# An attention loop in which the next batch's preparation runs three more steps ahead

## The chip, the cores and the metric

The kernel runs on one core of one Trainium2 chip. The metric is the device time of one execution in microseconds (us); lower is better. Engines are named as the profile names them: PE (TensorE; PEld is its weight loading), DVE (VectorE), ACT (ScalarE), POOL (GpSimd), SP (the queue that starts DMAs).

## What is computed

Six blocks on x of shape (4, 512, 128), in the order A B A C D C: a mixture of experts (A), eight layers of linear attention (B), A again, an attention block with its own experts (C), a state-space scan (D), and C once more. The change touches the attention in C, which runs twice:

```python
h = _layernorm(_layernorm(x), ln1_w, ln1_b)
h = causal depthwise convolution of h, 3 taps
q, k, v = split(h @ attn_w)               # 16 heads of width 8
q = q * cos + rotate_half(q) * sin        # the same for k
scores = where(causal, q @ k.T / sqrt(8), -1e30)
p = softmax(scores)
x = x + (p @ v) @ proj_w                  # then a norm and 4 experts
```

## The kernel before

Every engine has its own instruction stream, written out by hand, and engines wait for one another on semaphores. In the attention (lines 1245 to 1770) each of the 4 batches has two kinds of work.

**Side work** prepares a batch: 60 products of PE that take turns on two PSUM banks (`side`, line 1289 on), where product n waits until what lay in its bank two products before has been read. For each of the four query tiles i of 128 rows: `qkv` i; then DVE turns the positions in (`rope`, L1626 to L1633, among it the copy of v into the values' operand `vc`, L1629) and splits the numbers into bf16 pieces (`rest` L1638, `part3` L1644 and L1646), ACT rounds (`part` 1 and 2, L1417), POOL copies pieces (`spread` 1: three copies; `spread` 2: two copies). PE then transposes `key` i and `query` i (8 transposes each, L1314); ACT copies the keys (`copied`, L1427) and half of the queries (`odd_queries`, L1434), DVE the other half (`queries`, L1651). `max` products (L1325, L1329) fill a bank with scores, whose row maxima DVE takes (`maxima`, L1660): 4 for tile 0, 8 for tile 1, 16 each for tiles 2 and 3. With the maxima (`max_rows`) PE transposes the queries once more (`again` i), and ACT copies them.

**Main work** goes in 16 steps j (head group j // 4, key tile k = j % 4): `scores` (L1345) of 512 - 128 k columns in two halves on four banks, `exps` on ACT (L1479, two instructions), `select` on POOL (L1581, two), `values` on PE (L1355). A half of `scores` waits for the `exps` of the step before, which reads the same banks; `exps` j waits for `values` j - 2; `values` j waits for both `select` of j. After each group ACT copies the sums (`summed`, L1487), for which the first `values` of the next group wait; `turned` on PE, `normed` and `added_back` on DVE finish a batch.

While batch b's main work runs, the side work of batch b + 1 is dealt out over its 16 steps: side step j (a fixed list on each engine) goes with main step j. Batch 0's side work runs alone ahead of the loop, and batch 3's main work has none beside it but parts of the norm that follows. The order within a step before:

- PE: `scores` j + 1, side step j, `values` j, `turned`
- ACT: `exps` j, `summed`, side step j
- POOL: both `select` of j, side step j
- DVE: `normed`, side step j

Of the kernel before, what the change touches and what calls it, by code (L numbers as in the profile page):

```python
# [13 lines left out]
P = 128  # L14
# [41 lines left out]
def build(nc, x_in, pack_a, pack_b, pack_c, params, consts, out, stages="ABACDC"):  # L56
    par_at, par_cols = columns(PARAMS)
    con_at, con_cols = columns(CONSTS)
    with ExitStack() as ctx:
# [92 lines left out]
        vc = [view(4096 + 2048 * s, TPB, HEADS, 32) for s in range(2)]  # L152
        kt_s = [view16(8192 + 2048 * s, PAIRS, SEQ) for s in range(2)]
# [1121 lines left out]
        USES_BY_STEP = [2, 4, 9, 13, 18, 23, 26, 29, 37, 43, 47, 49, 55, 59, 60, 60]  # L1275
# [12 lines left out]
        def pe_attention(pe, c):  # L1288
# [60 lines left out]
            def values(b, j):  # L1349
# [3 lines left out]
                pe.wait_ge(S["sel_ok"], 32 * q + 2 * j + 2)  # L1353
                for m in range(4):
                    mm = pe.matmul(ps[32 * m:32 * m + 32, 4, k * P:SEQ], vc[b % 2][:, k, 4 * g + m, :],  # L1355
                                   pt[:, (2 * j + m // 2) % NPT, m % 2, 0:SEQ - k * P], start=(k == 0),
                                   stop=(k == TPB - 1), skip_group_check=True)
# [17 lines left out]
            pe.wait_ge(S["pad_ok"], c["attn"] + 1)  # L1375
            for n in range(USES):
                side(0, n)
            pe.wait_ge(S["ln_out"], 4 * c["ln"] + NB)
            scores(0, 0)
            for b in range(NB):  # L1380
                for j in range(STEPS):
                    if j + 1 < STEPS:
                        scores(b, j + 1)
                    if b + 1 < NB:
                        for n in range(USES_BY_STEP[j - 1] if j else 0, USES_BY_STEP[j]):
                            side(b + 1, n)
                        if j + 1 == STEPS:
                            scores(b + 1, 0)
                    values(b, j)
                    if b == LATE:  # L1390
# [16 lines left out]
        def act_attention(act, c):  # L1407
# [30 lines left out]
            def side(b, j):  # L1438
# [3 lines left out]
                elif j == 1:  # L1442
                    part(b, 0, 2)
                    part(b, 1, 2)
                    if b == 0:
                        act_first(act, c, 3)
                    copied(b, "key", 0)
                    odd_queries(b, 0)
                elif j == 2:
                    part(b, 2, 1)  # L1450
                elif j == 3:
                    part(b, 2, 2)
                    copied(b, "key", 1)
                    odd_queries(b, 1)
                    copied(b, "again", 0)
                elif j == 4:
                    part(b, 3, 1)
                elif j == 5:
# [3 lines left out]
                elif j == 6:  # L1462
                    copied(b, "again", 1)
                elif j == 8:
                    copied(b, "key", 3)
                    odd_queries(b, 3)
                elif j == 10:
                    copied(b, "again", 2)
                elif j == 14:
# [32 lines left out]
            for j in range(STEPS):  # L1502
                side(0, j)
                if j < NB - 1:
# [714 lines left out]
```

## Time and profile before

| | us |
|---|---|
| median of 3 runs | 2120.73 |
| lowest and highest of them | 2113.12, 2126.63 |
| the profiled execution | 2111.17 |
| its span, first to last instruction | 2109.4 |

The profile is that of one execution. Its span is cut below into stretches of the first attention: the side work of one batch ends with the transposes of `again` 3, and the stretch from there to the end of the next batch's `again` 0 is called a head here; the stretch from that `again` 0 to that batch's `again` 3 a body. So a round of the loop is a body and a head. Busy times of an engine add up its instructions without overlap; the clock is the mean share of full speed that TensorE was granted.

### The profile page before, as it was taken

How to read it: one execution, taken by the hardware profiler on the slowest of the kernel's cores; microseconds unless marked ns; L12 is line 12 of the kernel's file. 1: busy time of each engine (PE TensorE's matmuls, PEld its weight loads, DVE VectorE, ACT ScalarE, POOL GpSimd, SP SyncE). 2: the span in 40 equal slices, each digit the busy share in tenths (PEclk: the TensorE clock that was granted, in tenths of full speed). 3: DMA queues.
4: the chain of work that ended last, by engine and by line, in shares of the span. 5: the costliest groups of instructions: out<-in, count | busy, mean ns of one | idle time of the engine just before them, and what ended most of it. 6: DMA issues, size and time to landing. Idle time of an engine off the chain costs nothing.

```text
span 2109.4 us, 24691 instructions
## 1 busy us (share of the span) xinstructions
PE 1770.9 (84%) x8806; PEld 1110.2 (53%) x8806; DVE 1530.9 (73%) x2489; ACT 1334.9 (63%) x2121; POOL 654.1 (31%) x731
## 2 busy tenths in 40 slices
PE   8999798898898889996677789995776677777998
PEld 6887466665566558883233326881222232232786
DVE  6888687778787668878666545875998855664686
ACT  6998577767777679995355565556544345556554
POOL 1444111101111014445422231221898522223131
PEclk9999899999999979998899999997899679999999
DMA  3221000000000003210000001100000000000110
GB/s 100 75 76 52 15 18 18 1 18 18 18 18 11 0 13 104 70 61 15 1 1 1 1 1 46 65 1 9 3 3 32 0 1 1 1 1 1 56 56 21
DMA packets 23770, 52.89 MB, mean 25 GB/s; under 512 B 2336, under 2 KB 6816, under 8 KB 23648
## 3 DMA queue, kind: packets, MB, share of 16 engines
q1 hardware_dynamic: 23648, 51.30, 7.7%
q8 instruction: 71, 1.16, 0.2%
q14 instruction: 51, 0.42, 0.1%
HBM read 49.66 MB, written 1.64 MB: 24 GB/s over the span
## 4 chain that ended last, share of the span: by engine, by line
PE 56%; DVE 22%; ACT 16%; issue 4%; POOL 2%; DMA 1%; POOLq 0%; ACTq 0%; DVEq 0%; SPq 0%
PE ps L553 9%; PE ps L555 9%; PE ps L554 9%; DVE arena L1940 5%; DVE arena L1660 5%; PE ps L1355 3%; PE ps L782 3%; PE ps L785 3%; PE ps L1325 3%; ACT arena L1479 2%; PE ps L783 2%; PE ps L1314 2%; ACT arena L1427 2%; PE ps L1345 2%; DVE arena L1931 1%
## 5 line engine op out<-in xcount | busy, mean ns | idle before, releaser
L664 DVE TENSOR_TENSOR hid_lo<-arena,hid_hi 128x512 fp32r<-128x512 f32 x384 | 339.3, 896 | 66.9 <-ACT arena L613 65.4
L1660 DVE TENSOR_REDUCE arena<-ps 128x1 f32<-128x512 f32 (+3 forms) x352 | 213.4, 639 | 87.3 <-PE ps L1329 84.4
L553 PE MATMUL ps<-x_hi,w_hi 128*128 128x512 f32 x512 | 209.9, 410 | 2.0 <-DVE arena L756 2.0
L1581 POOL TENSOR_SCALAR_AFFINE_SELECT arena<-arena 128x256 f32<-128x256 f32 x256 | 108.2, 430 | 314.2 <-ACT arena L1479 311.7
L554 PE MATMUL ps<-x_lo,w_hi 128*128 128x512 f32 x512 | 204.0, 398 | 0.0
L555 PE MATMUL ps<-x_hi,w_lo 128*128 128x512 f32 x512 | 204.0, 398 | 0.0
L610 ACT ACTIVATE hid_hi<-ps,wslot 128x512 fp32r<-128x512 f32 x256 | 177.3, 693 | 33.7 <-PE ps L555 6.3
L1479 ACT ACTIVATE arena<-ps 128x1024 f32<-128x1024 f32 (+3 forms) x256 | 166.2, 705 | 50.0 <-PE ps L1345 49.5
L1325 PE MATMUL ps<-arena 128*128 128x512 bf16 (+3 forms) x512 | 133.7, 327 | 69.4 <-DVE arena L1660 37.8
L613 ACT ACTIVATE arena<-ps,wslot 128x512 f32<-128x512 f32 x256 | 175.0, 684 | 0.0
L1427 ACT ACTIVATE arena<-ps 128x1024 bf16<-128x1024 bf16 x64 | 65.5, 1024 | 149.8 <-PE ps L1314 149.7
L634 POOL TENSOR_TENSOR x<-x,arena 128x512 f32<-128x512 f32 x64 | 108.5, 1699 | 145.8 <-DVE arena L625 145.8
L553 PE MATMUL ps<-hid_hi,w_hi 128*128 128x512 f32 x384 | 151.6, 395 | 2.1 <-DVE hid_lo L664 2.1
L555 PE MATMUL ps<-hid_hi,w_lo 128*128 128x512 f32 x384 | 151.7, 395 | 0.0
L554 PE MATMUL ps<-hid_lo,w_hi 128*128 128x512 f32 x384 | 150.4, 392 | 0.0
L1957 POOL TENSOR_TENSOR arena<-arena 128x512 f32<-128x512 f32 x64 | 136.1, 2166 | 44.4 <-ACT arena L1882 44.4
L735 ACT ACTIVATE arena<-ps 128x512 f32<-128x512 f32 x128 | 76.4, 597 | 97.4 <-PE ps L555 97.3
L1325 PEld LDWEIGHTS ps<-arena 128*128 128x128 bf16 x512 | 42.6, 101 | 161.6 <-DVE arena L1660 98.6
L1345 PE MATMUL ps<-arena 50*128 50x256 bf16 (+3 forms) x512 | 68.3, 321 | 60.6 <-ACT arena L1479 58.0
L756 DVE TENSOR_TENSOR arena<-arena,ps 128x512 f32<-128x512 f32 x128 | 87.4, 683 | 38.6 <-ACT arena L735 38.5
L1355 PE MATMUL ps<-arena 128*32 128x512 f32 (+3 forms) x1024 | 109.1, 501 | 7.1 <-POOL arena L1581 5.1
L553 PEld LDWEIGHTS ps<-x_hi,w_hi 128*128 128x128 f32 x512 | 98.3, 192 | 29.3 <-DVE arena L756 5.2
(309 smaller groups left out, 4190.7 us busy)
## 6 DMA issues: line engine op xcount, KB each, us to landing
arena<-gates_dram SPq DMA_DIRECT2D x96, 256.0 KB, 3.5
wslot<-pack_a SPq DMA_DIRECT2D x16, 514.5 KB, 3.8
wslot<-pack_b SPq DMA_DIRECT2D x8, 900.5 KB, 4.6
wslot<-pack_c SPq DMA_DIRECT2D x8, 768.0 KB, 4.5
res<-x_in SPq DMA_DIRECT2D x4, 256.0 KB, 5.0
out_dram<-res SPq DMA_DIRECT2D x4, 256.0 KB, 2.9
con<-consts_dram SPq DMA_DIRECT2D x1, 559.0 KB, 3.9
bc_dram<-arena SPq DMA_DIRECT2D x1, 384.0 KB, 3.2
```

Source lines behind the costliest of these rows:

```text
L553: pe.matmul(ps[:, bank, :], w1, hi, start=start, stop=False)
L554: pe.matmul(ps[:, bank, :], w1, lo, start=False, stop=False)
L555: return pe.matmul(ps[:, bank, :], w2, hi, start=False, stop=stop)
L610: act.activation(hid_hi[item % 2][:, k, :], ps[:, k, :], ACT.Gelu, bias=bias)
L613: act.activation(hid32[:, k, :], ps[:, k, :], ACT.Gelu, bias=bias).then_inc(S["hi_ok"], 1)
L664: dve.tensor_tensor(hid_lo[item % 2][:, k, :], hid32[:, k, :], hid_hi[item % 2][:, k, :].bitcast(F32), ALU.subtract).then_inc(S["hid_ok"], 1)
L1325: pe.matmul(ps[:, bank, m * keys:(m + 1) * keys], qt_s[h % 2][:, h // 2, i * P:(i + 1) * P], kt_s[b % 2][:, h // 2, 0:keys], start=(m == 0 ...
L1345: mm = pe.matmul(ps[:, 2 * r + jj, 0:n], kt_s[b % 2][r0:r0 + MROWS, hp, k * P:(k + 1) * P], q2_s[b % 2][r0:r0 + MROWS, hp, k * P:SEQ], sta ...
L1355: mm = pe.matmul(ps[32 * m:32 * m + 32, 4, k * P:SEQ], vc[b % 2][:, k, 4 * g + m, :], pt[:, (2 * j + m // 2) % NPT, m % 2, 0:SEQ - k * P], ...
L1479: act.activation(pt[:, u % NPT, :, 0:n], ps[:, 2 * r:2 * r + 2, 0:n], ACT.Exp, scale=SCALE).then_inc(S["exp_ok"], 1)
L1660: dve.tensor_reduce(neg_max[:, i, heads[0]:heads[-1] + 1:step], ps[:, bank, 0:len(heads) * keys].rearrange("p (m k) -> p m k", k=keys), AX ...
L1957: pool.tensor_tensor(ch[:, s, t, :], hst[:, s, t, :], c_s[:, u % 2, :], ALU.mult).then_inc(S["ch_ok"], 1)
```

## The change

On every engine side step j + 3 goes with main step j, so that the last three main steps of a batch carry side steps 0, 1 and 2 of the batch after the next, and side steps 0 to 2 of batch 1 run ahead of the loop. Side work of batch b + 2 thus begins while batch b's values are still in use, for which the values' operand gets a third buffer, in the norm's `rstd`; POOL fills its unused columns after the convolution. The side lists are dealt out a little differently over the steps. The new order within a step (`ahead` gives side step j + 3):

- PE: `scores` j + 1, `values` j, side step j + 3, `turned`
- ACT: `summed`, `exps` j + 1, side step j + 3; `exps` 0 of a batch comes behind the last side step of the batch before
- POOL: both `select` of j, side step j + 3
- DVE: `normed`, side step j + 3

```diff
+        vc.append(rstd[:, :, :].rearrange("p i (h d) -> p i h d", d=32))
...
-        USES_BY_STEP = [2, 4, 9, 13, 18, 23, 26, 29, 37, 43, 47, 49, 55, 59, 60, 60]
+        USES_BY_STEP = [2, 2, 5, 9, 13, 18, 23, 26, 29, 36, 41, 44, 48, 53, 58, 60]
+        LEAD = 3
+
+        def ahead(b, j):
+
+            return [(b + 1 + (j + LEAD) // STEPS, (j + LEAD) % STEPS)] if b + 1 + (j + LEAD) // STEPS < NB else []
...
+                if (b, j) == (2, 0):
+                    pe.wait_ge(S["pad_ok"], 2 * c["attn"] + 2)
...
+            for j in range(STEPS):
+                side_step(0, j)
+            side_step(1, 0)
             pe.wait_ge(S["ln_out"], 4 * c["ln"] + NB)
             scores(0, 0)
+            for j in range(1, LEAD):
+                side_step(1, j)
             for b in range(NB):
                 for j in range(STEPS):
                     if j + 1 < STEPS:
                         scores(b, j + 1)
-                    if b + 1 < NB:
-                        for n in range(USES_BY_STEP[j - 1] if j else 0, USES_BY_STEP[j]):
-                            side(b + 1, n)
-                        if j + 1 == STEPS:
-                            scores(b + 1, 0)
+                    elif b + 1 < NB:
+                        scores(b + 1, 0)
                     values(b, j)
+                    for at in ahead(b, j):
+                        side_step(*at)
...
                 elif j == 1:
                     part(b, 0, 2)
                     part(b, 1, 2)
-                    if b == 0:
-                        act_first(act, c, 3)
+                elif j == 2:
                     copied(b, "key", 0)
                     odd_queries(b, 0)
-                elif j == 2:
                     part(b, 2, 1)
                 elif j == 3:
                     part(b, 2, 2)
+                elif j == 4:
                     copied(b, "key", 1)
...
+            side(1, 0)
             for b in range(NB):
+                exps(b, 0)
+                if b == 0:
+                    for j in range(1, LEAD):
+                        side(1, j)
                 for j in range(STEPS):
-                    exps(b, j)
                     if j % TPB == 0 and 4 * b + j // TPB:
                         if j:
                             summed(b, j // TPB - 1)
                         else:
                             summed(b - 1, 3)
+                    if j + 1 < STEPS:
+                        exps(b, j + 1)
                     if b and j == 4:
                         y_turned(b - 1)
-                    if b + 1 < NB:
-                        side(b + 1, j)
-                    else:
+                    for at in ahead(b, j):
+                        side(*at)
...
-            SPREAD_BY_STEP = {0: [(0, 1), (1, 1)], 1: [(0, 2), (1, 2)], 2: [(2, 1)], 3: [(2, 2)], 4: [(3, 1)], 5: [(3, 2)]}
+            SPREAD_BY_STEP = {0: [(0, 1), (1, 1)], 1: [(0, 2), (1, 2)], 2: [(2, 1)], 3: [(2, 2)], 5: [(3, 1)], 6: [(3, 2)]}
...
+            pool.memset(vc[2][:, :, :, DH:DH + 1], 1.0)
+            pool.memset(vc[2][:, :, :, DH + 1:32], 0.0).then_inc(S["pad_ok"], 1)
+            side(1, 0)
+            for j in range(1, LEAD):
+                side(1, j)
...
-                if i == 0 and q >= 2:
-                    dve.wait_ge(S["pv_mm"], 16 * (q - 1))
+                if i == 0 and b == 3:
+                    dve.wait_ge(S["pv_mm"], 16 * (q - 2))
...
-                dve.tensor_copy(vc[b % 2][:, i, :, 0:DH], ps[:, bank, 2 * P:3 * P].rearrange("p (h d) -> p h d", d=DH))\
+                dve.tensor_copy(vc[b % 3][:, i, :, 0:DH], ps[:, bank, 2 * P:3 * P].rearrange("p (h d) -> p h d", d=DH))\
...
                 elif j == 1:
                     part3(b, 0)
                     part3(b, 1)
-                    if b == 0:
-                        dve_second(dve, c, 1)
+                elif j == 2:
                     queries(b, 0)
-                elif j == 2:
                     rope(b, 2)
+                elif j == 3:
                     maxima(b, 0, range(4))
                     rest(b, 2)
                     max_rows(b, 0)
-                elif j == 3:
+                elif j == 4:
                     part3(b, 2)
                     queries(b, 1)
                     rope(b, 3)
...
-                if j < 2:
-                    dve_first(dve, c, j + 2)
-                elif j < 4:
-                    dve_second(dve, c, j)
+                if j in (0, 2):
+                    dve_first(dve, c, 2 + j // 2)
+                elif j in (1, 3, 4):
+                    dve_second(dve, c, {1: 1, 3: 2, 4: 3}[j])
+            for j in range(LEAD):
+                side(1, j)
```

The rest of the lists moves the same way, to side steps one later than before (`key`, `query` and `again` 1 from 3 to 4, `key` 3 from 8 to 9), with at most 5 maxima in a step.

## Rows read from the trace of the kernel before

**Rows 1.** First line of the page: the span of the profiled execution.
```profile
span 2109.4 us, 24691 instructions
```

**Rows 2.** Busy times by stretch, first attention: stretch, length, engines (instructions), clock, DMA.
```profile
1022.35:1047.52 25.17, 17.09 (x116) 7.46 (x120) 12.19 (x36) 12.36 (x19) 8.03 (x23) 0.80 0.00 1
1047.52:1092.60 45.08, 34.16 (x292) 13.90 (x296) 29.61 (x60) 23.84 (x34) 10.23 (x27) 0.96 0.00 1
1092.60:1117.28 24.68, 17.10 (x136) 8.06 (x140) 12.74 (x38) 13.40 (x22) 8.79 (x25) 0.86 0.00 1
1117.28:1163.98 46.70, 36.07 (x298) 14.45 (x302) 30.30 (x61) 24.33 (x35) 10.24 (x27) 0.96 0.01 1
1163.98:1188.84 24.86, 17.21 (x137) 8.10 (x140) 12.77 (x38) 13.40 (x22) 8.80 (x25) 0.86 0.00 1
1188.84:1234.24 45.40, 34.61 (x298) 14.20 (x302) 30.17 (x61) 24.33 (x35) 10.24 (x27) 1.00 0.00 1
1234.24:1236.15 1.91, 1.00 (x13) 0.31 (x12) 0.00 (x0) 1.58 (x4) 0.51 (x2) 1.00 0.00 0
1236.15:1276.41 40.26, 32.45 (x232) 9.96 (x230) 13.87 (x27) 29.29 (x49) 15.89 (x33) 0.87 0.00 1
```

**Rows 3.** Timeline in head 1: start, us, engine, line, count, [idle <-releaser].
```profile
1097.72 0.42 DVE L1626 TENSOR_TENSOR arena<-ps,con 128x256 f32<-128x256 f32 x1 [5.27 <-PE ps L1302]
...
1098.77 0.43 DVE L1633 TENSOR_TENSOR arena<-arena 128x256 f32<-128x256 f32 x1
...
1100.65 0.42 ACT L1417 ACTIVATE arena<-arena 128x256 bf16<-128x256 f32 x1 [1.00 <-DVE arena L1633]
1100.97 1.49 ACT L1479 ACTIVATE arena<-ps 128x768 f32<-128x768 f32 x2
1101.12 0.66 POOL L1558 COPY arena<-arena 128x256 bf16<-128x256 bf16 x1 [0.36 <-ACT arena L1417]
...
1101.82 0.35 PE L1345 MATMUL ps<-arena 50*128 50x256 bf16 x2 [2.50 <-ACT arena L1479]
1102.21 0.77 POOL L1581 TENSOR_SCALAR_AFFINE_SELECT arena<-arena 128x256 f32<-128x256 f32 x2
```

**Rows 4.** Waits within 1094.5 to 1165.9: engine, line, releaser, us in total, times, longest.
```profile
DVE arena L1660 <- PE ps L1329: 11.9, 13, 3.0
...
PE ps L1345 <- ACT arena L1479: 7.9, 10, 2.5
```

**Rows 5.** Groups by line, 1094.5 to 1165.9: count, busy us, mean ns, idle before.
```profile
L1581 POOL TENSOR_SCALAR_AFFINE_SELECT arena<-arena 128x256 f32<-128x256 f32 x33 | 13.2, 409 | 41.8 <-ACT arena L1479 41.5
...
L1479 ACT ACTIVATE arena<-ps 128x1024 f32<-128x1024 f32 x9 | 8.8, 1022 | 2.3 <-PE ps L1345 2.3
...
L1427 ACT ACTIVATE arena<-ps 128x1024 bf16<-128x1024 bf16 x8 | 8.2, 1024 | 17.3 <-PE ps L1314 17.3
...
L1487 ACT ACTIVATE arena<-ps 128x512 f32<-128x512 f32 x4 | 2.4, 605 | 0.0
...
L1638 DVE TENSOR_TENSOR arena<-arena 128x256 f32<-128x256 f32 x4 | 1.8, 440 | 0.1
```

**Rows 6.** Timeline of PE in body 2, at the full clock.
```profile
1139.88 1.20 PE L1314 MATMUL ps<-ident,arena 128*128 128x128 bf16 x16
...
1143.28 1.06 PE L1355 MATMUL ps<-arena 128*32 128x512 f32 x8
```

**Rows 7.** Timeline of PE in head 1 (the last row after the clock is back).
```profile
1103.77 1.81 PE L1314 MATMUL ps<-ident,arena 128*128 128x128 bf16 x15
1105.51 1.51 PE L1355 MATMUL ps<-arena 128*32 128x384 f32 x8
...
1115.58 0.91 PE L1302 MATMUL ps<-par,res 128*128 128x384 f32 x2 [0.67 <-ACT arena L1427]
```

**Rows 8.** Timeline of DVE, six maxima in a row.
```profile
1155.29 3.75 DVE L1660 TENSOR_REDUCE arena<-ps 128x1 f32<-128x512 f32 x6 [0.91 <-PE ps L1329]
```

**Rows 9.** Timeline of POOL, filling the unused columns of one buffer.
```profile
957.36 1.35 POOL L1589 MEMSET arena<- 128x1472 f32 x1
```

More of the change, by code:

```diff
@@ L1373, in turned, with side_step @@
                 mm.then_inc(S["t_mm"], 1)
-            pe.wait_ge(S["pad_ok"], c["attn"] + 1)
-            for n in range(USES):
-                side(0, n)
+            pe.wait_ge(S["pad_ok"], 2 * c["attn"] + 1)
+            def side_step(b, j):
+                for n in range(USES_BY_STEP[j - 1] if j else 0, USES_BY_STEP[j]):
+                    side(b, n)
+            for j in range(STEPS):
+                side_step(0, j)
+            side_step(1, 0)
             pe.wait_ge(S["ln_out"], 4 * c["ln"] + NB)
             scores(0, 0)
+            for j in range(1, LEAD):
+                side_step(1, j)
             for b in range(NB):
@@ L1455, in side @@
                     copied(b, "again", 0)
-                elif j == 4:
+                elif j == 5:
                     part(b, 3, 1)
-                elif j == 5:
+                elif j == 6:
                     part(b, 3, 2)
@@ L1582, in pool_attention @@
                                            channel_multiplier=-1).then_inc(S["sel_ok"], 1)
-                    if b + 1 < NB:
-                        side(b + 1, j)
+                    for at in ahead(b, j):
+                        side(*at)
         def pool_pads(pool, c):
-            for v in vc:
+            for v in vc[0:2]:
                 pool.memset(v[:, :, :, DH:DH + 1], 1.0)
@@ L1702, in side @@
                     queries(b, 2)
[L1703 removed]
+                elif j == 7:
                     maxima(b, 2, range(2))
[L1705 removed]
+                elif j == 8:
                     maxima(b, 2, range(2, 5))
[L1707 removed]
+                elif j == 9:
                     maxima(b, 2, range(5, 8))
                     queries(b, 3)
[L1710 to L1718 removed]
+                    maxima(b, 2, range(8, 10))
+                elif j == 10:
+                    maxima(b, 2, range(10, 15))
+                elif j == 11:
+                    maxima(b, 2, range(15, 16))
+                    max_rows(b, 2)
+                    maxima(b, 3, range(2))
                 elif j == 12:
[L1720 removed]
+                    maxima(b, 3, range(2, 5))
                 elif j == 13:
[L1722 removed]
+                    maxima(b, 3, range(5, 10))
+                elif j == 14:
+                    maxima(b, 3, range(10, 15))
+                elif j == 15:
+                    maxima(b, 3, range(15, 16))
                     max_rows(b, 3)
@@ L1761, in dve_attention @@
                         added_back(b - 1)
-                    if b + 1 < NB:
-                        side(b + 1, j)
-                    else:
+                    for at in ahead(b, j):
+                        side(*at)
+                    if b == LATE:
                         if j - 1 in NORM_STEPS:
```

30 lines of the change are left out of this document (10 added, 20 removed).

## The prediction

> **What bounds the kernel now.** I read the page first: the profiled execution spans 2109.4 us [rows 1], and its time, 2111.2, lies 1.8 above that. Then I cut the attention by stretches [rows 2]. The reader should see that no engine is full. Body 2 lasts 46.70 us with PE busy for 36.07 and DVE for 30.30; the head before it lasts 24.68 with 17.10 and 12.74. A round of body and head takes 69.8 (45.08 + 24.68) or 71.6 (46.70 + 24.86), the last batch's main work alone 40.26. So the loop is set by chains from engine to engine, and a schedule decides it. The timeline in head 1 [rows 3] shows such a chain: `exps` 1 runs at 1100.97, right behind a `part` that had waited 1.00 us for DVE, and PE's `scores` have by then stood still for 2.50 us, waiting for that `exps`. Over a round PE's `scores` wait 7.9 us for `exps`, and DVE's maxima 11.9 us for their products [rows 4]. The first wait is what an `exps` put ahead of the side work could take away. The view by stretches also shows the clock: 0.80 to 0.86 of full speed in the heads, 0.96 to 1.00 in the bodies, so about 7 us of each head run at the lower of the two levels (24.7 x 0.14 x 2).
>
> **The change, part by part.** No product, reduction or exponential is added or removed; order changes, and two POOL fills are added. SP and its DMAs are not touched. So I follow the new queues, through a whole round, with the durations of the trace: a `select` pair 0.8, an `exps` of 1024 columns 1.02 (2.0 the pair), a copy of 8 transposes 1.02, `summed` 0.61, `rest` 0.44 [rows 5], 8 transposes 0.60 and `values` of 512 columns 1.06 [rows 6], `qkv` 0.8 in a row (0.91 with its load, [rows 7]), a maximum 0.63 in a row (3.75 / 6, [rows 8]); a `rope` from product to sum 1.48, `part` 0.42, three POOL copies 1.1 and from this two copies 0.7, as an estimate [rows 3]. A hop between engines costs about 0.05 (a `part` ends at 1101.07, POOL starts at 1101.12).
>
> *The body, side steps 5 to 15, main steps 2 to 12.* With five maxima a step lasts 3.65: `scores` and `values` 1.0, a first product 0.45, then DVE's pace. Before, DVE stood still 0.91 between two steps' maxima [rows 8]; now I find 0.6, for `values` no longer waits for the side products. But two steps pay for it elsewhere. Step 4 takes 6.1: `summed` 0 now stands on ACT behind the side step before it, two copies of 1.02, and `values` 4 waits for it 1.1 us; then `exps` 5, `y_turned` and the copy of `again` 1 hold up a product of maxima. Step 6 takes 5.5: `key` 3 must drain two maxima, then two copies of 1.02 follow one another. Step 3, with three maxima, `key` 2 and `query` 2, takes 4.45, step 9, with the copy of `again` 2 in its middle, 4.3, steps of two or three maxima, or of five short ones, 2.85 to 3.25. The eleven steps come to 0.6 + 3.65 + 4.45 + 6.1 + 3.1 + 5.5 + 3.25 + 2.85 + 4.3 + 3.65 + 3.7 + 3.7 = 44.85 at the full clock (the 0.6 is a `turned`), some 2 less where no batch is being finished (no `y_turned`, no projection). Before: 45.08 (none being finished), 46.70 and 45.40 [rows 2]. Gain 2.2 + 1.85 + 0.55 = 4.6 in an attention.
>
> *The head, side steps 0 to 4, now main steps 13, 14, 15, 0 and 1.* This is where the change costs. Times from the end of `again` 3: its copy ends at 1.1 and frees the bank of `qkv` 1; `rope` 0 and `part` follow `qkv` 0 and end at 3.8, the second pair at 5.2. POOL now has the three copies of both tiles between `select` 13 and `select` 14: `select` 14 ends at 7.15 (rows 3 show the same queue: a `select` at 1102.21 right behind copies). Two copies for each tile, then `select` 15 to 9.25, `values` 15 to 9.7, `key` 0 to 10.3, its copy to 11.35, `qkv` 2 to 12.15, `rope` 2 to 13.7, `part` to 14.15. **On ACT, `exps` 0 of the next batch stands behind that `part`**, since side step 2 goes with main step 15 and `exps` 0 comes after it: 16.15, `summed` 16.75, `values` 0 to 17.8. Only then come the four products of tile 0's maxima, now behind `values` 0 on PE: last drained 21.0, `rest` 21.4, `part` 21.85, POOL's copies 22.55, and behind these `select` 1, 23.35. `values` 1, `key` 1 and `query` 1 to 25.4, a copy and the odd queries' copy, `again` 0 to 27.6. Before: 24.68 and 24.86 [rows 2]. Where side and main work ran beside each other, they now stand in one chain: +2.9 and +2.75. Head 0, ahead of the loop, has no `values` 14 to wait for: by the same steps 26.05, against 25.17, and 1.0 more because batch 0's first maxima now stand behind a piece of the norm on DVE (`dve_first` of tile 3): +1.9.
>
> *The end of the third round.* From `again` 3 to the last batch's first `exps` were 1.91 [rows 2]; three bare main steps, with two `exps` ahead of it, make this 2.95: +1.05. The last batch's order changes only on ACT, where norm instructions change places with `exps`: its 40.26 I leave as they are (bounds -2 and +2: what `exps` 8 gains there, `summed` behind the norm loses).
>
> *What costs nothing by itself.* The third buffer removes a wait that did not bind (`rope` 0 waited for PE's product, 5.27 us idle, [rows 3]) and is only what lets side step 0 start early; its fills, 1.35 us and a short one [rows 9], lie on POOL between the convolution and the first copies of batch 1, which wait for DVE and ACT; uncovered they would cost 1.6 once in an attention.
>
> *The clock.* The sums for the new order are at the full clock, those of before are not. In head 1, 15 transposes took 1.81 where 16 take 1.20 at the full clock, and `values` of 384 columns 1.51 [rows 6, 7], where 1.06 for 512 lets one expect 0.8: about 1.4 on the path. Between nothing and the whole head at the lower level (some 8.3 us of PE work on its path, by the transposes' 0.6 more for each: 5.0) I take 1.4, for the new head too has PE idle in pieces of up to 4 us: 3 x 1.4 = 4.2.
>
> The sum for one attention: -4.6 + 2.9 + 2.75 + 1.9 + 1.05 + 4.2 = +8.2; it runs twice: +16.4. On the profiled execution 2127.6; the runs' median, 2120.7, lies 9.6 above that execution, so I give **2137**, 0.8% more.
>
> **Rivals.**
>
> *A: the waits go and nothing takes their place (faster).* The 7.9 us in which `scores` wait for `exps` [rows 4] vanish from three rounds: 2 x 3 x 7.9 = 47, 2073. For it: that wait is what `exps` a step ahead aims at, and no engine is full. Against it: `exps` 0 of each batch is not ahead but behind a side step, and the head, where the longest of these waits lie [rows 3], is there. It decides if the head stays under 22 us. The Trainium skill would lean this way (Perfetto Trace Analysis, Optimization Strategy: find the gaps of the contended engine and make what ends them start sooner); by it the sum would be A's. The order of the queues in the head speaks against it.
>
> *B: the clock sinks through the whole head (slower).* If PE's idle pieces keep the lower level all through a head of 27.6 us, it costs 5.0 instead of 1.4: 6 x 3.6 = 22 more, 2159. For it: heads are where the clock is down now [rows 2]. Against: PE still works in most of the head's 2 us pieces. It decides where the granted clock of a head falls under about 0.7. The Trainium skill has this as a rule (TensorE: Matmul & The Clock Gate, Loop structure matters more than you think): a loop that lets PE wait between products runs them cold. The trace agrees that the level falls in the head, not how far it would fall.
>
> *C: no effect.* Side work sets the round in both orders, so where it starts does not matter: head and body as before, within 6 us, 2121. For it: body sums so close to the old ones. Against: two `select`, `exps` 0 and `values` 0 that stand newly in the side chain.
>
> **How the numbers follow.** Forecast 0.60, A 0.12, B 0.16, C 0.12. One per cent, 21 us, is about what a measurement of this kernel can tell from no change. The forecast's own range is 2115 to 2152 (its clock at nothing or at twice 1.4, the last batch at its bounds); 0.42 of its 0.60 lies within 1%, 0.18 above. So faster 0.12, same 0.42 + 0.12 = 0.54, slower 0.18 + 0.16 = 0.34. The range must reach B, and below it takes in no clock loss (2129), bodies whose 0.6 us of DVE idle vanish too (ten such steps in an attention: -12 in all), the last batch at -2 (-4) and the 6 us by which the runs of before lie off their median: 2107 to 2165. It leaves out A.
>
> **What would show it.** Right: heads of 26 to 29 us and bodies of 43 to 45; ACT's `exps` 0 of a batch right behind a `part` that waited for DVE; POOL's `select` 14 behind copies; no wait of `scores` in the bodies over 1 us. Wrong: `exps` 0 running while side step 2 waits; a body under 41, which would mean that `summed` holds nothing up; heads near 22.

## The result, and the profile after

The changed kernel takes **2144.40 us** (median of 4 runs, 2141.64 to 2146.97) against 2117.07 (4 runs, 2113.12 to 2126.63): ratio **1.0118**, 95% interval 1.0089 to 1.0148 (the two medians by themselves give 1.0129). It is slower by 1.2%; the forecast was 2137, 0.8% slower, in a range of 2107 to 2165. Its chances, by a line at 1%, were 0.54 for "same" and 0.34 for "slower"; by that line it is slower. The profiled execution took 2145.15, span 2143.4; 34.0 us more span than in the profiled execution of before [rows 1], which lies 5.9 below the median of its kernel.

The same view by stretches as in [rows 2], for the first attention. Columns: stretch, its length, then busy us (instructions) of PE, PE's weight loads, DVE, ACT and POOL, then granted clock, DMA share and GB/s. In order: batch 0's side work alone, then head and body three times, the tail (from the third round's `again` 3 to the first `exps` of the last batch), the last batch's main work.

```profile
990.29:1028.15 37.86, 27.44 (x145) 10.79 (x146) 29.43 (x56) 7.88 (x9) 24.02 (x22) 0.68 0.00 0
1028.15:1057.38 29.23, 18.62 (x101) 8.24 (x100) 12.27 (x35) 11.69 (x17) 7.21 (x21) 0.62 0.00 1
1057.38:1101.33 43.95, 32.81 (x284) 13.14 (x288) 29.09 (x59) 23.61 (x34) 10.04 (x27) 0.96 0.00 1
1101.33:1133.37 32.04, 20.82 (x134) 9.54 (x135) 12.84 (x37) 13.71 (x22) 8.67 (x25) 0.73 0.00 1
1133.37:1177.48 44.11, 33.04 (x295) 13.71 (x296) 30.31 (x62) 24.00 (x35) 10.04 (x27) 1.00 0.00 1
1177.48:1209.49 32.01, 20.59 (x135) 9.22 (x135) 12.95 (x38) 13.71 (x22) 8.67 (x25) 0.68 0.00 1
1209.49:1253.60 44.11, 33.04 (x295) 13.71 (x296) 30.11 (x61) 24.00 (x35) 10.04 (x27) 1.00 0.00 1
1253.60:1257.17 3.57, 3.09 (x32) 1.08 (x32) 0.55 (x2) 2.67 (x6) 1.53 (x4) 1.00 0.00 0
1257.17:1295.24 38.07, 29.76 (x232) 9.54 (x230) 13.82 (x27) 29.35 (x49) 14.86 (x32) 0.96 0.00 1
```

Against [rows 2], the account of both attentions (us; "said" is the prediction's term for one attention):

| stretch | said | first | second |
|---|---|---|---|
| batch 0's side work, from its first `qkv` | 0 | +5.3 | +2.7 |
| three heads | +11.75 (4.2 of it the clock) | +18.6 | +17.5 |
| three bodies | -4.6 | -5.0 | -8.0 |
| tail | +1.05 | +1.7 | +1.7 |
| last batch | 0 | -2.2 | -2.1 |
| sum | +8.2 | +18.4 | +11.7 |

Outside the attentions 3.9 more, which says nothing of the change: in the traces of this case the first attention's first `qkv` starts anywhere from 963.4 to 969.0, though nothing ahead of it was edited. The three bodies together gain what was said in the first attention (-1.1, -2.6 and -1.3 where -2.2, -1.85 and -0.55 were said), and more in the second; the heads lose half as much again, and there the granted clock is 0.62 to 0.73, where it was 0.80 to 0.86.

The timeline in head 2 (from 1177.48): start, us, engine, line, count, and in brackets the idle time before and who ended it. L1320 is the transposes, L1331 the products of the maxima, L1351 `scores`, L1363 `values`, L1431 `part`, L1492 `exps`, L1579 and L1582 POOL's copies, L1607 `select`.

```profile
1180.45 0.29 PE L1351 MATMUL ps<-arena 50*128 50x128 bf16 x4
1182.87 0.66 POOL L1579 COPY arena<-arena 128x256 bf16<-128x256 bf16 x1 [0.36 <-ACT arena L1431]
1184.09 0.86 POOL L1607 TENSOR_SCALAR_AFFINE_SELECT arena<-arena 128x256 f32<-128x256 f32 x2
1185.01 1.08 PE L1363 MATMUL ps<-arena 128*32 128x256 f32 x8 [4.27 <-POOL arena L1607]
1187.57 1.89 PE L1320 MATMUL ps<-ident,arena 128*128 128x128 bf16 x16
1192.91 0.42 ACT L1431 ACTIVATE arena<-arena 128x256 bf16<-128x256 f32 x1 [2.20 <-DVE arena L1659]
1193.35 1.94 ACT L1492 ACTIVATE arena<-ps 128x1024 f32<-128x1024 f32 x2
1195.87 1.94 PE L1363 MATMUL ps<-arena,rstd 128*32 128x512 f32 x8
1199.55 0.61 PE L1331 MATMUL ps<-arena 128*128 128x128 bf16 x4
1200.41 0.40 PE L1331 MATMUL ps<-arena 128*128 128x128 bf16 x4
```

The chain is the one that was written down by hand: `select` 14 behind POOL's copies, `exps` 0 (1193.35) right behind a `part` that had waited 2.20 for DVE, `values` 0 after it. But PE's pieces are long: 16 transposes 1.89 where they took 1.20 at the full clock [rows 6], `values` of 512 columns 1.94 against 1.06. PE stands still for 4.27 us behind `select` 14. The granted clock falls within that stop (1.00 from 1182 to 1183, 0.50 from 1184 on), and all PE rows from there to 1200 have the long durations; the four products at 1200.41 are back at 0.40 from 0.61. Some 20 us of this head lie at the lower of the two levels (32.0 x 0.32 x 2) and 17 of head 1, where before it were about 7.

In head 1 of before the level fell behind a stop too, the one of 2.50 [rows 3], but was back after some 7 us. What PE did in between differs. Here is head 2 of the kernel after from 1185 on:

```profile
1185.00:1200.20 15.20, 11.44 (x65) 4.57 (x65) 3.45 (x9) 6.29 (x8) 3.34 (x11) 0.50 0.00 0
```

And head 1 of before, behind its stop:

```profile
1104.00:1108.00 4.00, 4.00 (x28) 2.24 (x27) 0.68 (x1) 3.13 (x4) 0.56 (x2) 0.50 0.01 2
1108.00:1112.00 4.00, 2.88 (x22) 1.54 (x21) 3.06 (x9) 0.96 (x3) 0.96 (x3) 0.91 0.00 0
```

In the old head PE then worked for four microseconds without a gap, and the level came back. In the new one it was busy for 11.44 of 15.20 us, with one more stop, of 3.06 us behind `exps` 0, and the level stayed at 0.50. The old heads 1 and 2 have one long stop of PE each (2.50; the next is 0.91), the new ones three (4.3, 3.1, and 2.7 or 2.9).

### The profile page after: what moved, and what is told of

It is laid out like the page before. It is cut to its first block, busy times and chain, and to the rows that moved or that the text cites. A ratio compares the mean times of both kernels' runs of the same rounds, so it can differ in the third digit from the quotient of the medians.

```text
span 2143.4 us, 24673 instructions
## 1 busy us (share of the span) xinstructions
PE 1780.4 (83%) x8787; PEld 1117.8 (52%) x8806; DVE 1532.6 (72%) x2489; ACT 1334.1 (62%) x2121; POOL 654.4 (31%) x735
## 4 chain that ended last, share of the span: by engine, by line
PE 57%; DVE 21%; ACT 15%; issue 3%; POOL 2%; DMA 1%; POOLq 0%; DVEq 0%; ACTq 0%; SPq 0%
PE ps L554 9%; PE ps L556 9%; PE ps L555 9%; DVE arena L1686 5%; DVE arena L1969 5%; PE ps L1363 4%; PE ps L1331 3%; PE ps L783 3%; PE ps L786 3%; PE ps L784 2%; ACT arena L1441 2%; PE ps L1320 2%; PE ps L1351 2%; ACT arena L1492 2%; DVE arena L1960 1%
## 5 line engine op out<-in xcount | busy, mean ns | idle before, releaser
L1686 DVE TENSOR_REDUCE arena<-ps 128x1 f32<-128x512 f32 (+3 forms) x352 | 214.4, 639 | 121.4 <-PE ps L1335 119.5
L1492 ACT ACTIVATE arena<-ps 128x1024 f32<-128x1024 f32 (+3 forms) x256 | 165.9, 702 | 102.9 <-PE ps L1351 102.4
L1331 PE MATMUL ps<-arena 128*128 128x128 bf16 (+3 forms) x498 | 135.7, 343 | 64.2 <-DVE arena L1686 36.7
L1607 POOL TENSOR_SCALAR_AFFINE_SELECT arena<-arena 128x256 f32<-128x256 f32 x256 | 105.4, 423 | 218.2 <-ACT arena L1492 216.4
L1986 POOL TENSOR_TENSOR arena<-arena 128x512 f32<-128x512 f32 x64 | 136.1, 2165 | 45.9 <-ACT arena L1911 45.9
L1441 ACT ACTIVATE arena<-ps 128x1024 bf16<-128x1024 bf16 x64 | 65.6, 1025 | 132.1 <-PE ps L1320 132.0
L1331 PEld LDWEIGHTS ps<-arena 128*128 128x128 bf16 x512 | 45.2, 106 | 183.2 <-DVE arena L1686 103.5
L1363 PE MATMUL ps<-arena 128*32 128x512 f32 (+3 forms) x768 | 82.4, 504 | 51.6 <-POOL arena L1607 38.4
L554 PEld LDWEIGHTS ps<-x_hi,w_hi 128*128 128x128 f32 x512 | 98.1, 192 | 29.2 <-DVE arena L757 5.1
L635 POOL TENSOR_TENSOR hb<-hb,arena 128x512 f32<-128x512 f32 x32 | 42.1, 1316 | 225.0 <-DVE arena L629 225.0
```

The source lines that it names most:

```text
L554: pe.matmul(ps[:, bank, :], w1, hi, start=start, stop=False)
L635: pool.tensor_tensor(dst[:, t, :], dst[:, t, :], gated[:, item % 2, :], ALU.add).then_inc(S["added"], 1)
L1331: pe.matmul(ps[:, bank, m * keys:(m + 1) * keys], qt_s[h % 2][:, h // 2, i * P:(i + 1) * P], kt_s[b % 2][:, h // 2, 0:keys], start=(m == 0 ...
L1492: act.activation(pt[:, u % NPT, :, 0:n], ps[:, 2 * r:2 * r + 2, 0:n], ACT.Exp, scale=SCALE).then_inc(S["exp_ok"], 1)
L1686: dve.tensor_reduce(neg_max[:, i, heads[0]:heads[-1] + 1:step], ps[:, bank, 0:len(heads) * keys].rearrange("p (m k) -> p m k", k=keys), AX ...
L1986: pool.tensor_tensor(ch[:, s, t, :], hst[:, s, t, :], c_s[:, u % 2, :], ALU.mult).then_inc(S["ch_ok"], 1)
```

## The experiments

**1. Does the clock alone make the heads longer than said?** The theory: the order's chain is 27.6 us, as said, and the other 4.4 are the lower clock. The rivals: the clock is low but lies off the path; or the chain itself is longer. In `e2_warm` PE's idle pieces in the head are filled with products whose results are overwritten unread.

```diff
+            def warm(bank, n):
+                for _ in range(n):
+                    pe.matmul(ps[:, bank, :], ident16[:, :], mask_qk16[:, :].unsqueeze(1).to_broadcast([P, TPB, P]),
+                              start=True, stop=True, skip_group_check=True)
...
+                    if b + 2 < NB and j == 14:
+                        warm_keys(b + 2, 17)
```

(17 of them ahead of `values` 14, 12 ahead of `scores` 1, 11 ahead of `values` 1.)

> The changed kernel, plus small products of PE whose results are overwritten unread: 17 before values 14, 12 before scores 1, 11 before values 1 of a batch, in the pieces where PE stands idle in a head (on a bank that is free by then). Nothing else differs. In the changed kernel the heads last 32.0 us at a granted clock of 0.68 to 0.73, the bodies 44.1. Theory (order and clock): 27.6 us of a head are the chain at the full clock and about 4.4 are PE work at the lower clock. With PE kept busy the clock goes to 0.9 or more and the heads to 27 to 29 us; the whole falls by 2 x 3 x 3 to 4.4, some 18 to 26 us. Rival 1 (clock alone): without the clock the heads are as before, 24 to 25 us. Rival 2 (clock off the path): the clock rises and the heads stay at 31 to 33 us.

2125.3 us, with 2112.2 for the kernel before on the same chip. Stretches of head 1, body 2 and head 2, then PE in head 2, which starts at 1170.66 (L1390 is the added products):

```profile
1098.87:1126.56 27.69, 23.40 (x174) 10.44 (x175) 12.87 (x38) 13.72 (x22) 8.71 (x25) 1.00 0.01 1
1126.56:1170.66 44.10, 33.04 (x294) 13.70 (x296) 30.10 (x61) 24.00 (x35) 10.09 (x27) 1.00 0.00 1
1170.66:1198.31 27.65, 23.40 (x175) 10.43 (x175) 12.87 (x38) 13.72 (x22) 8.71 (x25) 1.00 0.00 1
```

```profile
1173.84 3.84 PE L1390 MATMUL ps<-mask_qk,ident 128*128 128x512 bf16 x17
1178.19 0.64 PE L1363 MATMUL ps<-arena 128*32 128x256 f32 x8 [0.51 <-POOL arena L1634]
1187.43 1.06 PE L1363 MATMUL ps<-arena,rstd 128*32 128x512 f32 x8 [0.19 <-ACT arena L1527]
```

The heads fall from 32.0 to 27.65 and 27.69, the body stays where it was. The chain now runs as forecast almost to the tenth: `values` 15 ends 9.7 us after the start of the head (said 9.7), `qkv` 2 at 12.3 (said 12.15), `values` 0 at 17.8 (1187.43 + 1.06 - 1170.66; said 17.8; 20.3 in the kernel after), the head at 27.65 (said 27.6). Both rivals fall. The whole, one run, is 19 us below the changed kernel's median (said 18 to 26). More work, and less time: the lower clock costs 4.4 us in each of the two later heads and 4.1 in head 0 (29.2 to 25.15), where 1.4 was said.

**2. Who holds `values` 0?** The prediction put the head's loss at one place on ACT: `exps` 0 stands behind the side step's `part`. `e1_exp0_first` takes it, and the `summed` before it, in front.

```diff
-                exps(b, 0)
                 if b == 0:
+                    exps(b, 0)
...
-                    if j % TPB == 0 and 4 * b + j // TPB:
...
+                    if j and j % TPB == 0:
+                        summed(b, j // TPB - 1)
                     if j + 1 < STEPS:
                         exps(b, j + 1)
+                    elif b + 1 < NB:
+                        exps(b + 1, 0)
+                        summed(b, 3)
```

> The changed kernel, but on ACT exps 0 of the next batch and the last summed of this one stand ahead of side step 2 instead of behind it. The prediction named exps 0 behind a part on ACT as the place where the head costs. If that queue alone holds values 0, the head loses exps and summed, 2.6 us, from 32.0 to about 29.4. Theory from the trace of the changed kernel: no gain by itself, for values 0 also waits for select 0, which stands on POOL behind the copies of the same part; and the copy of key 0 now comes 1 us later behind exps and summed: heads of 32 to 33.5 us, bodies 44.1.

2145.8 us (before 2112.2): nothing gained; heads 29.6, 31.7 and 31.0. The timeline in head 2:

```profile
1193.59 0.42 ACT L1431 ACTIVATE arena<-arena 128x256 bf16<-128x256 f32 x1 [1.47 <-DVE arena L1659]
1194.03 1.51 ACT L1492 ACTIVATE arena<-ps 128x768 f32<-128x768 f32 x2
1194.41 0.54 POOL L1582 COPY arena<-arena 128x128 bf16<-128x128 bf16 x2
1194.89 0.77 POOL L1607 TENSOR_SCALAR_AFFINE_SELECT arena<-arena 128x256 f32<-128x256 f32 x2
1195.76 1.93 PE L1363 MATMUL ps<-arena,rstd 128*32 128x512 f32 x8 [3.28 <-issue]
```

`exps` 0 is done, and what runs behind the `part` is already `exps` 1 (768 columns). But `select` 0 stands in POOL's queue behind the copies of that same `part`, and `values` 0 starts 0.1 us after its end (1194.89 + 0.77; the bracket at `values` 0 names no releaser). The wait had only changed queue. `e1b_exp0_select0_first` moves both:

```diff
+            select(0, 0)
...
+                    if j:
+                        select(b, j)
+                    if j + 1 == STEPS and b + 1 < NB:
+                        select(b + 1, 0)
                     for at in ahead(b, j):
                         side(*at)
```

> As the run before, and on POOL select 0 of the next batch stands ahead of the copies of side step 2 as well. Theory: now values 0 is out of the chain from part 1 of tile 2, the products of tile 0's maxima follow qkv 2 on PE after scores 1 and values 0: the head loses 2.5 to 3.7 us at the full clock, more where this keeps the clock up: 27 to 29.5 us, the whole 10 to 20 us less than the changed kernel. Rival (the chain runs through side work alone, so main work's place in it does not matter): heads stay at 31 to 33 us.

2127.8 us, and the two later heads fall to 27.57 and 27.58, by 4.4 to 4.5 each, with the clock still low:

```profile
1101.34:1128.91 27.57, 19.26 (x135) 8.81 (x135) 12.87 (x38) 13.71 (x22) 8.67 (x25) 0.75 0.00 1
```

So the serial chain that was named is real, but it goes through two in-order queues, and mending ACT's alone leaves it standing (POOL's alone was not run).

**3. Which part of the change costs, which gains?** The change has three parts: the exponentials a step ahead, `values` ahead of the side products, and the lead (side work three steps ahead, with its third buffer and its new side lists). The first two are tried alone on the kernel before, then together; the lead alone was not run. `e5_exp_ahead_alone` only puts the exponentials a step ahead (`e5_again` is the same kernel, with six runs):

```diff
+                exps(b, 0)
                 for j in range(STEPS):
-                    exps(b, j)
...
+                    if j + 1 < STEPS:
+                        exps(b, j + 1)
```

> The kernel before with one part of the change alone: on ACT exps j + 1 ahead of side step j (and exps 0 of a batch behind side step 15, which is empty). No lead, two buffers, products of PE in the old order. In the kernel before heads last 24.7 us, bodies 45.1 to 46.8, and scores wait 7.9 us a round for exps. Theory (the lead is what puts main work into the side chain; exps ahead by itself only takes waits away): bodies of 43.5 to 45 us, heads of 23 to 25, the whole 5 to 20 us less than before. Rival (exps ahead is what puts ACT's summed and copies late): bodies of 46 us or more, heads of 26 or more.

> The kernel before with exps a step ahead alone, as in the look before (2097 us against 2118), timed with rounds. Theory (exps ahead by itself takes waits away, the lead gives them back): 0.985 to 0.995 of the kernel before. Rival (the look was within what two runs differ by): 0.997 or more.

2097.3 us against 2118.1, then 2096.04 (2092.43 to 2099.67) against 2115.8: ratio **0.9891, 0.9858 to 0.9925**. The first of these parts is a gain of 1.1% by itself. Head 1 and body 2 of `e5_again`, and PE's wait for `exps` in that body:

```profile
1091.68:1116.73 25.05, 15.89 (x137) 7.24 (x140) 12.81 (x38) 14.61 (x23) 9.29 (x27) 0.93 0.00 1
1116.73:1160.39 43.66, 35.68 (x299) 14.65 (x302) 30.20 (x61) 23.11 (x35) 9.37 (x26) 0.96 0.01 2
```

```profile
PE ps L1345 <- ACT arena L1479: 0.6, 1, 0.6
```

In the body of before that wait is 3.2 us. This body shrinks by 3.0, this head grows by 0.4 (25.05 against 24.68); the other two heads of this attention are longer than before by about 1, the other bodies shorter by 4.4 and 2.1.

`e6_values_first_alone` only puts `values` ahead of the side products on PE; `e7_both_no_lead` does both, with neither lead nor third buffer.

```diff
+                    elif b + 1 < NB:
+                        scores(b + 1, 0)
+                    values(b, j)
                     if b + 1 < NB:
...
-                        if j + 1 == STEPS:
-                            scores(b + 1, 0)
-                    values(b, j)
```

> The kernel before with another part alone: on PE values j ahead of side step j, exps in place and no lead. Theory: values then wait for a select whose exps has only just ended, about 0.8 us a step, and the side products wait behind them: rounds 4 to 12 us longer than the 71.5 of before, the whole 20 to 70 us more. Rival (values first by itself closes DVE's idle pieces): bodies of 44 us, the whole within 10 us of before or less.

> The kernel before with exps a step ahead and values ahead of the side step, but no lead and two buffers: the change without its lead. Theory: bodies as in the changed kernel, 43.5 to 45 us; in the head no exps 0 stands behind part 1 of tile 2, but values 1 to 3 stand between the side products of tiles 0 and 1: heads of 24.5 to 28 us, less than the changed kernel's 32. The whole between 10 us less and 10 us more than before. Rival (the lead does not matter, the other two parts lengthen the head): heads of 30 us or more.

2195.4 and 2113.1 us against 2118.1. `values` first alone costs 77 us, more than the 20 to 70 expected. One body and ACT's longest wait there, both of `e6`:

```profile
1140.76:1195.98 55.22, 42.09 (x292) 15.98 (x292) 29.80 (x61) 24.12 (x35) 10.24 (x27) 0.81 0.00 1
```

```profile
ACT arena L1427 <- PE ps L1314: 19.0, 5, 7.5
```

That wait (of `copied` for the transposes) was 12.1 in body 2 of before: `values` j wait for `exps` j, the transposes now stand behind them on PE, the copy behind the transposes, and `exps` j + 1 behind the copy on ACT (the ring is read from the order of the queues). The exponentials a step ahead open this ring again (`e7`, bodies of 42.65 to 45.6), but `values` first still costs 16 us beside `e5`.

`e3_side_first` and `e4_exp_in_place` go the other way: the changed kernel with the side step ahead of `values` again, and with `exps` back in place.

```diff
+                    for at in ahead(b, j):
+                        side_step(*at)
                     values(b, j)
-                    for at in ahead(b, j):
-                        side_step(*at)
```

```diff
-                exps(b, 0)
...
                 for j in range(STEPS):
+                    exps(b, j)
...
-                    if j + 1 < STEPS:
-                        exps(b, j + 1)
```

> The changed kernel with one of its parts undone: on PE the side step stands ahead of values again. Theory: in the head the maxima of tile 0 no longer stand behind values 0, nor key 1 behind values 1 and its select: heads 3.5 to 4.5 us shorter, 27.5 to 28.5; in the bodies DVE's idle piece between two steps' maxima grows by 0.3 us in some ten steps: 45 to 47 us instead of 44.1. Together a round 1 to 3 us shorter, the whole 5 to 15 us less. Rival (values first is what shortened the bodies by more, and the head does not depend on it): heads 32, bodies 46 to 47, the whole 10 us more.

> The changed kernel with exps back in place on ACT (exps j, summed, side step j + 3): the lead and the order on PE stay. Theory: exps 0 stays behind side step 2, and exps 1 falls behind part 2 of tile 2: heads of 32 to 34 us; in the bodies scores wait for exps again: 45 to 48 us instead of 44.1; the whole 8 to 25 us more than the changed kernel. Rival (exps ahead buys nothing in the bodies): bodies of 44 us, the whole as the changed kernel.

2121.9 (before 2112.2) and 2216.35 (before 2118.1). Head 1 and body 2 of `e3`:

```profile
1094.03:1120.56 26.53, 18.51 (x136) 8.30 (x140) 12.96 (x38) 13.71 (x22) 8.67 (x25) 0.81 0.00 1
1120.56:1167.64 47.08, 35.02 (x296) 14.23 (x302) 30.78 (x61) 24.00 (x35) 10.04 (x27) 0.96 0.00 1
```

Side first gives 5.5 us in each of the two later heads and 8.9 in head 0, and takes 1.9 to 3.9 back in each body. `e4` was expected 8 to 25 us above the changed kernel and lies 71 above it (98.3 over the kernel before against 27.3): in its first attention the two later heads are 35.8, the bodies 49.5 to 53, the tail 7.47. The exponentials ahead are therefore worth 71 us within the new order and 21 in the old one. The difference goes with `values` first and not with the lead: without the lead, beside `values` first, they are worth 82 (`e6` to `e7`).

The parts read together, each as us against the kernel before (all but the last from single runs, each with one run of before on the same chip; those two gave 2112.2 and 2118.1, and 14 runs on another chip 2111.65 to 2133.74, so these are good to some 6 us at best): exponentials ahead -21; with `values` first -5; with the lead but side first +10; all three +27. The lead costs some 25 to 31 beside `exps` ahead alone, and about 32 where `values` go first. The two sums are alike, but they lie in different places. Over both attentions, `e3` beside `e5_again` has bodies longer by 29 in sum and heads shorter by 8; the kernel after beside `e7` has heads longer by 25 and bodies shorter by 1.

**4. Can the lead pay?** `e10_lead_mended` is the changed kernel with the order mended on three queues (side step first on PE; `exps` 0 and `select` 0 first, with `summed` left behind). `e11_head_side_first` mends the head alone: the same two moves on ACT and POOL, but PE's side step goes first only with main steps 15, 0 and 1, as here:

```diff
+                    side_first = j in (0, 1, STEPS - 1)
+                    for at in ahead(b, j) if side_first else []:
+                        side_step(*at)
                     values(b, j)
-                    for at in ahead(b, j):
+                    for at in [] if side_first else ahead(b, j):
                         side_step(*at)
```

> The changed kernel with its lead kept and its head mended as far as the order allows: on PE the side step ahead of values, on ACT exps 0 and on POOL select 0 of the next batch ahead of side step 2 (summed stays behind it). Theory: the head falls from 26.5 us (side step first alone) to 22 to 25.5; the bodies stay at 47 to 48, since the lead puts the side steps beside other main steps: the whole 2100 to 2118 us. Rival (heads of 26.5 are set by the side work alone): heads of 26 to 27, the whole as with the side step first alone, 2122.

> The changed kernel with lead and exps ahead, exps 0 and select 0 of the next batch ahead of side step 2, and on PE the side step ahead of values in main steps 15, 0 and 1 alone (the head), behind values in all others (the bodies). Theory: heads as with the lead mended, 21.5 to 24.5 us, bodies as in the changed kernel, 44 to 45; a round of 66 to 69 us against 71.5 before: 2080 to 2098 us, 0.98 to 0.99 of before. Rival (the short heads and the short bodies were not independent: what a head leaves undone the body pays): bodies of 46 us or more, 2100 us or more.

2110.65 us (one run) against 2115.8 for `e10`, then 2096.82 (2096.08 to 2100.7) against 2116.78 for `e11`: ratio **0.9912, 0.9891 to 0.9934**. Head 1, body 2 and head 2 of `e11`:

```profile
1088.75:1110.15 21.40, 14.70 (x128) 7.14 (x132) 12.77 (x38) 13.60 (x22) 8.71 (x25) 0.92 0.01 1
1110.15:1155.19 45.04, 34.25 (x305) 14.02 (x306) 30.20 (x61) 24.12 (x35) 10.09 (x27) 1.00 0.01 1
1155.19:1178.44 23.25, 16.79 (x128) 7.86 (x132) 12.99 (x38) 13.60 (x22) 8.71 (x25) 0.78 0.00 1
```

These heads are shorter than those of before by 3.3 and 1.6, and the body is 45.0 where `e10`, side first throughout, has 45.8 to 47.2 in its first attention. With the head mended the lead pays, yet it only draws level with `e5`, one moved line: the two intervals overlap. Over both attentions its heads are 22 us shorter than those of `e5_again` and its bodies 13 longer, its tails 2 longer each; the rest of the difference lies in batch 0's side work, whose time changes with its clock from run to run (see the last section). Both beat the kernel before and the changed one.

**5. A miss.** The idea was that `qkv` 2 is what is late in the head of `e5`; `e9_qkv2_earlier` is `e5` with this product a side step earlier.

```diff
-        USES_BY_STEP = [2, 4, 9, 13, 18, 23, 26, 29, 37, 43, 47, 49, 55, 59, 60, 60]
+        USES_BY_STEP = [2, 5, 9, 13, 18, 23, 26, 29, 37, 43, 47, 49, 55, 59, 60, 60]
```

> The same, and the product qkv of tile 2 one side step earlier on PE (ahead of values 1 instead of behind it, turned and scores 3). Theory (the head is a side chain in which main work stands): values 1, turned and scores 3 come out of the chain between the copy of key 0 and rope of tile 2: heads of 23 to 24.5 us instead of 25.8, 6 of them, 7 to 15 us less than exps ahead alone. Rival (DVE or ACT is late for that rope anyway): heads of 25.5 to 26 us.

2103.74 us, ratio 0.9929 (0.9903 to 0.9955): no better than `e5`, and heads of 26.6, 27.25 and 26.6 where shorter ones were expected. The timeline in its head 2 (L1302 is `qkv`, L1367 `turned`, L1734 `normed`, L1628 `rope`):

```profile
1176.10 1.65 PE L1302 MATMUL ps<-par,res 128*128 128x384 f32 x2 [0.26 <-ACT arena L1427]
1179.11 0.90 PE L1367 MATMUL ps<-con,arena 128*128 128x128 f32 x4
1180.05 0.26 DVE L1734 RECIPROCAL arena<-ps 128x16 f32<-128x16 f32 x1 [3.49 <-PE ps L1367]
1180.55 0.41 DVE L1628 TENSOR_TENSOR arena<-ps,con 128x256 f32<-128x256 f32 x1
```

The product is done at 1177.75, but DVE takes it at 1180.55: its `rope` stands behind `normed`, which waited 3.49 us for `turned`, and `turned` now stands on PE behind the very product that was moved up, which runs at the lower clock.

## Why the prediction was right, and where its sum was not

*Direction and mechanism: right.* The bodies gain, the heads pay more, and the heads' price is one serial chain of side and main work, which `e2_warm` shows at its forecast length. Of what "would show it right", the bodies (42.7 to 44.1, said 43 to 45), `exps` 0 behind the `part`, and `select` 14 behind copies are there, and PE's waits in body 2 hold no `scores`. The four longest of six (L1331 is the products of the maxima, L1320 the transposes, L1363 `values`; L1686 the maxima, L1441 `copied`, L1698 `max_rows`, L1500 `summed`):

```profile
PE ps L1331 <- DVE arena L1686: 4.2, 13, 0.5
PE ps L1331 <- ACT arena L1441: 2.4, 3, 1.0
PE ps L1320 <- DVE arena L1698: 1.4, 1, 1.4
PE ps L1363 <- ACT arena L1500: 1.2, 1, 1.2
```

The last of these is `values` 4 behind `summed` 0: 1.2, said 1.1. DVE's idle time between two steps' maxima, 0.91 before [rows 8], was said to be 0.6; one such place in body 2:

```profile
1171.26 3.16 DVE L1686 TENSOR_REDUCE arena<-ps 128x1 f32<-128x512 f32 x5 [0.58 <-PE ps L1335]
```

Only the heads, 29 to 32 us, are outside their 26 to 29.

*The term that was mis-sized: the clock.* 1.4 us for each head, 4.2 for an attention; 4.4 in two heads and 4.1 in the third by `e2_warm`, 12.8 for an attention. That is rival B's mechanism, which the prediction put at 5.0 a head and gave 0.16. The step that failed is "the new head too has PE idle in pieces of up to 4 us": it took the new head for one like the old, with its one long stop of 2.50 [rows 3], after which the level came back. In the new head the stop behind `select` 14 (4.27) comes first and two more follow; the level does not come back until 1200 in head 2, and in head 1 it is back from 1115 to 1118 and falls again. So nearly all PE work on the chain had the long durations, not two pieces of it. The Trainium skill (TensorE: Matmul & The Clock Gate, Loop structure matters more than you think) says that a loop with a long wait for a DMA between every two products runs them cold. Here the long waits are for POOL and ACT, and the traces agree: 0.68 in the head as it is, 1.00 with its waits filled. That any wait between products would do it, as the prediction put the rule, they do not show: body 2, with PE's waits of up to 1.4 us, kept 1.00.

*The place of the head's loss: half right.* That `exps` 0 stands behind side step 2 on ACT was named as the cause; taking it away alone gave nothing (2145.8), since the same order on POOL holds `select` 0. The hand-made chain would have shown it: POOL's queue stands in it with copies ahead of `select` 1, but it was not run again with `exps` 0 moved.

*The heads without the clock.* In `e2_warm` the three heads are 5.8 us longer than before, where 7.55 were said.

*Head 0 and batch 0's side work.* The 1.9 said for head 0 is not there: 25.15 at the mended clock against 25.17. Of it, the 1.0 for the piece of the norm ahead of batch 0's first maxima lies earlier, and is larger. Batch 0's first maxima (L1686), on DVE behind two steps of the norm:

```profile
981.67 0.82 DVE L321 TENSOR_TENSOR sq<-sq,rstd 128x512 f32<-128x512 f32 x1
982.42 0.77 DVE L322 TENSOR_TENSOR hb<-xc,rstd 128x512 f32<-128x512 f32 x1
983.22 2.69 DVE L1686 TENSOR_REDUCE arena<-ps 128x4 f32<-128x512 f32 x4
```

From batch 0's first `qkv` to its `again` 0 are 22.9 and 22.8 us where they were 21.0 and 21.3. What follows, to `again` 3, grew by 3.4 and 1.1, with the clock at 0.68 in the first. But the kernel before itself took 34.4 in its first attention and 37.3 in its second, `e5_again`, whose order there is that of before, 34.4 and 39.0, and `e7` and `e9`, with that order too, 38.4 in their first. So neither the 3.4 nor the 1.1 can be put down to the change.

*Last batch.* Said unchanged, measured -2.2. Its PE was busy for 29.76 us at a clock of 0.96, against 32.45 at 0.87 [rows 2]; `e2_warm`, with the new order there, took 40.13 at 0.87. The gain goes with the clock, not with the order.

*The fills* cost nothing, as said: they end at 1019.50, and POOL's next instruction, the first copy of batch 1, comes after 12.06 us of idle time, waiting for ACT.

```profile
1018.16 1.34 POOL L1597 MEMSET rstd<- 128x1472 f32 x1
1031.57 0.40 POOL L1579 COPY arena<-arena 128x256 bf16<-128x256 bf16 x1 [12.06 <-ACT arena L1431]
```

*The rivals.* A (the waits vanish, 2073) names a real gain but overrates it: `exps` ahead alone takes 3.2 us of that wait in body 2 down to 0.6 and brings 20 to 23 us, not 47. B came with its mechanism (heads at 0.62 to 0.73) but not with its time, 2159. C (no effect) falls: bodies and heads moved, in opposite directions.

*The number and luck.* By the spans the change cost 34.0 us, twice the 16.4 of the sum, and the heads' clock alone accounts for 17 of the difference (twice 12.8 - 4.2). That the time came out only 7 above the forecast is in part luck: the profile of before, from which the account is taken, was one of its kernel's shorter executions, and the forecast stood on a median of three runs, 2120.7, that a fourth brought down to 2117.07; from there the same terms give 2133.5. Batch 0's side work and the last batch moved by 5.3 and -2.2 in the first attention, where 1.0 (counted under head 0) and nothing were said, and partly cancel. One sum on the range is off as well: the clock at nothing or at twice 1.4 (8.4 either way) and the last batch at its bounds (4) give 2125 to 2149 around 2137, and not 2115 to 2152; the wider range, 2107 to 2165, does not rest on it.

*What stays open.* Why the bodies are 2 to 4 us longer with the lead and the side step first (`e3`, `e10`) than with `values` first was not tried. Read from the trace, some 2 of the 3 us in body 2 of `e3` are one stop: a product of maxima, there ahead of `values` 4 on PE, waits 2.8 us for an ACT copy that stands behind `summed`, `exps` 5 and `y_turned` (the longest wait of this kind is 1.0 in the kernel after). Whether the new side lists cost or gain anything by themselves, apart from the lead, was not tried either.

## What to carry to other kernels

When an instruction is to run earlier, follow its product through every in-order queue up to the engine that waits for it: `exps` 0 moved on ACT alone gave nothing, with `select` 0 moved on POOL too it gave 4.5 us in each of the later heads. Test the parts of a bundled change apart: here one moved line is worth 1.1%, and the two parts added to it took that and 1.2% more. When a new order makes PE wait longer in one stretch, price it also with all PE work on the path behind that wait at the lower level's durations: here that bound, 5.0 us a head, was nearer to the measured 4.4 than the 1.4 read from the old order.

## What the runs showed of the hardware

Adding work made the kernel faster: some 40 unread products in each of the later heads (x174 instead of x134 PE instructions in head 1) took 4.4 us off a head of 32.0, and 19 off the whole, and the granted clock there rose from 0.68 or 0.73 to 1.00. The level also differs between stretches that run the same code: batch 0's side work in the kernel before, first and second attention, 144 PE instructions in each.

```profile
987.92:1022.35 34.43, 22.24 (x144) 9.26 (x144) 29.37 (x56) 7.88 (x9) 22.54 (x20) 0.95 0.00 0
1654.99:1692.25 37.26, 26.64 (x144) 10.02 (x144) 29.16 (x56) 7.88 (x9) 22.63 (x20) 0.73 0.00 1
```

One at 0.95, the other at 0.73 and 2.8 us longer, with the same DVE and ACT work: a difference of 2 to 3 us between such stretches says nothing of an edit until the granted clock beside it has been read. Why the level falls in one and not in the other was not tried.
